# Moving a wait for gate rows and one load of turned rows at the start of the early units

## The chip, the cores and the metric

The kernel runs on one NeuronCore of one Trainium2 chip. A NeuronCore has five engines with instruction streams of their own: TensorE (PE; its weight loads are listed as PEld), VectorE (DVE), ScalarE (ACT), GpSimd (POOL) and SyncE (SP). They are ordered only by semaphores. Transfers are issued by SyncE, ScalarE (ACTq) and GpSimd (POOLq) and carried out by sixteen DMA engines. The metric is the device time of one execution in microseconds, smaller is better; the time of a kernel is the median of its runs.

## The reference

For x of shape (4, 1024, 512), 4096 tokens in all, a modulated layer: six rows per batch come from `silu(c) @ wmod`, two of them gates.

```python
h = _layernorm(x) * (1 + ca) + sa
x = x + ga * attn_ref(h, ...)      # shift-mix time part, then channel part
h = _layernorm(x) * (1 + cb) + sb
x = x + gb * ffn_ref(h, ...)       # gb: the gate rows of this case

# ffn_ref: D = 512, F = 352, E = 8 experts, K = 2, shared width 704 = 2 * F
shared = (silu(x @ Wsg.T) * (x @ Wsu.T)) @ Wsd.T
scores = softmax(x @ Wr.T);  top 2 of 8, weighted by their scores
out_e  = (silu(x @ Wg[e].T) * (x @ Wu[e].T)) @ Wd[e].T
return routed + shared
```

## The kernel before

The 4096 tokens are 32 tiles of 128 rows. Stage 1 (the time part) and stage 2 (the channel part, the second layer norm, router logits and routing) go tile by tile. The feed-forward part is cut into units. A unit is one half (352 columns) of the shared network for one tile, or one tile of 128 routed rows for one expert. In a unit TensorE does `up` (24 products of 128x352 in banks PS_G and PS_U), ScalarE the `silu`, VectorE `hid` (the product of both), TensorE turns `hid` (`rows_turned`, L2067), ScalarE and VectorE split it in a high and a low part (`hid_hi` L1225, `hid_lo` L1658), and TensorE does `down` (9 products, L2072 to L2074). Products are made of three matmuls each, from float32r high and low parts (L573 to L575), so every operand has a high and a low tile.

The units come in four parts. **Fused**: units 0 to 29, the shared network for tiles 0 to 14 (FU = 15), run inside the steps of stage 2, four steps behind (LAG). **Early**: tiles 15 to 18 (`EARLY`, up to SPLIT = 19), two units each, after stage 2 has ended. **Routed**: 39 double tiles of 256 rows, each with its expert's weights. **Late**: shared units of tiles 19 to 31. This case acts at the seam of fused and early.

A shared unit reads its rows in turned form from DRAM, where ScalarE stored them (`store_turned`, `h3T_out`), into one of two tiles `ex_x_hl`. Fused units use `ex_x_hl[1]` alone (`fused_turned`, semaphore `sf_in`, L1234). Early units alternate (`load_turned`, `sx_in`, L1239): tile 15 slot 0, tile 16 slot 1. Slot 0 lies on the bytes of `x2_t`, which stage 2 reads until `xhat_2` of tile 31 in step 29; unit n runs in step n + 4. ScalarE issues these loads in `silu_of`, after the activation of every second unit. TensorE waits for them in `up` (L2152).

The gate rows `mod3` are four rows of 512, one for each batch, spread over all partitions by four loads of SyncE (L871, semaphore `mod3_in`). VectorE first multiplies with them in `base_of` (L1828), for tile 15; tiles to 14 use another copy, `gb_t`, in `base_fused` (L1676, L1679).

What matters around this is the order of VectorE's queue in `early_step`, since an engine runs its queue strictly in order. In each half: `hid_lo` of the unit before; routing pieces of the last group of tiles (BEFORE_HID); `hid` of this unit; in the first half `base_fused` or `base_of` of the tile before; more pieces (AFTER_HID). The pieces end in `expert_tables`, `tile_tables` (L1789 to L1796, releases `route_done`) and `result_slots`.

SyncE's queue at the seam, in order: the last rows to be scattered (`load_scattered`, L844, which wait for earlier scatters `sc_out`, then L862), the gate rows L871, residual rows of tiles 15 and 16 (L877), the store of tile 14 (L894), residual rows of 17 and 18 (L877, each waits for the landing of the one two before it), two more row loads (L862), `route_done`, the first expert's weights (L626 to L629), eight stores of zero rows behind the experts' regions (`pad_rows`, L888, `pad_out`), then, after waits for all scatters and all zero rows, the first expert's rows (L911) and the second expert's weights. GpSimd issues the scatters (L1048, L1089). ScalarE's first routed step has `expert_hi` of the second expert (L1307) ahead of the second half of the rows (L1298) and of `hid_hi`.

Of the kernel before, what the change touches and what calls it, by code (L numbers as in the profile page):

```python
# [23 lines left out]
B, T = 4, 1024  # L24
N = B * T
NT = N // P
# [10 lines left out]
FU = 15  # L37
# [82 lines left out]
EARLY = Part(FU, SPLIT, 0, FUSED)  # L120
# [4 lines left out]
def slot_of(part, n):  # L125

    return (n - part.first) % 2
# [60 lines left out]
def in_fused(v):  # L188
    return v.real() and v.n < 2 * FU
# [35 lines left out]
def build(nc, io, out):  # L225
# [16 lines left out]
    with ctx:  # L242
        def sem(name):
            return ctx.enter_context(nc.semaphore(name))
# [4 lines left out]
        def steps(name, *names):  # L249
            return Steps(sem(name), *names)  # L250
# [215 lines left out]
        mod3_in = sem("mod3_in")  # L466
# [44 lines left out]
        xh2_vec = steps("xh2_vec", "xhat")  # L511
# [601 lines left out]
        def _(act):  # L1113
# [113 lines left out]
            def silu(u, bank, follows=True):  # L1227
                if follows:
                    act.wait_ge(*u_vec.done(u - 1, "hid"))
                act.wait_ge(*u_pe.done(u, "up"))  # L1230
                act.activation(sg_t[:], PS_G[bank][:, 0:F], ACT.Silu).then_inc(u_act.sem, 1)  # L1231

            def fused_turned(n):
                act.dma_start(ex_x_hl[1][:].rearrange("p m c t -> p (m c t)").bitcast(F32),  # L1234
                              h3T_d[n * P:(n + 1) * P, :]).then_inc(sf_in, 16)

            def load_turned(part, n):
                slot = slot_of(part, n)
                act.dma_start(ex_x_hl[slot][:].rearrange("p m c t -> p (m c t)").bitcast(F32),  # L1239
                              h3T_d[n * P:(n + 1) * P, :]).then_inc(sx_in[slot], 16)  # L1240
# [11 lines left out]
            def silu_of(v):  # L1252
                if not in_fused(v):
                    return
                silu(v.n, 0, v.back(1).real())
                if v.p == 0:
                    return
                if v.pair is None and v.n == 2 * FU - 1:
                    act.wait_ge(*xh2_vec.done(NT - 1, "xhat"))
                    load_turned(EARLY, FU)  # L1260
                    load_turned(EARLY, FU + 1)
                else:
                    fused_turned(v.half + 1)

            def route_ones_of(t):
                if t.n == 2:
                    act.wait_ge(route_const, 4)
                    act.activation(ones[:], ones_made[:], ACT.Copy).then_inc(route_ones, 1)
                    act.activation(earlier[:], earlier_made[:], ACT.Copy).then_inc(route_ones, 1)
# [119 lines left out]
        def _(dve):  # L1389
# [424 lines left out]
            def pieces(table, t, half):  # L1814
                for piece in table.get(2 * (t.n - FU) + half, ()):
                    piece(*([LAST] if piece in (softmax_and_first, second, row_slots) else []))

            def hid_of(part, t, half):
                dve.wait_ge(*u_pe.done(part.unit(t, half) - 2, "turned"))
                hid_rows(part.unit(t, half), half, bank_of(part, half))  # L1820

            def hidlo(part, t, half):
                hidlo_rows(part.unit(t, half))

            def base_of(part, n):
                dve.wait_ge(*u_pe.done(part.unit(part.tile(n), 1), "down"))
                dve.wait_ge(*base_vec.done(n - 1, "base"))
                dve.tensor_tensor(gated_t[:], PS_Y[:], mod3[:, n // TPB, :], ALU.mult).then_inc(base_vec.sem, 1)  # L1828
                order = n - FU
                dve.wait_ge(sr_in[order % 2], 16 * (order // 2) + 16)  # L1830
                if n >= 2 * COMBINED_FIRST:
                    dve.wait_ge(*cb_vec.done(n // 2, "out"))
                dve.wait_ge(*base_vec.done(n, "gated"))
                dve.tensor_tensor(base[:, n, :], base[:, n, :], gated_t[:], ALU.add).then_inc(base_vec.sem, 1)
# [19 lines left out]
            def early_step(t):  # L1854
                for half in range(2):
                    hidlo(*EARLY.before(t, half))
                    pieces(BEFORE_HID, t, half)
                    if t.only(SPLIT - 1) and half:
                        expert_lo(FIRST, 0)
                    hid_of(EARLY, t, half)  # L1860
                    if not half:
                        if t.only(FU):
                            base_fused(FU - 1, 2 * FU - 1, True)
                            dve.wait_ge(mod3_in, 16 * B)
                        else:
                            base_of(EARLY, t.n - 1)
                    pieces(AFTER_HID, t, half)
                if t.only(SPLIT - 1):
                    x_lo(0, 0)
# [81 lines left out]
        def _(pe):  # L1951
# [169 lines left out]
            def rank_in_step(t):  # L2121
                g = group_at(t.n, 2)
                if g is not None:
# [4 lines left out]
                    rank(g)  # L2128

            lead, _, before_rank = in_turn((r2, 0), (k2, 0), (fused_up, LAG), (tk, 0), (t3, 2), (fused_down, LAG), (cv, 0))  # L2130
            _, _, after_rank = in_turn((router, 2), (t2, -2))

# [147 lines left out]
```

## Time and profile before

| | us |
|---|---|
| median of 3 runs | 1848.51 (1846.16 to 1848.79) |
| the profiled execution | 1840.96 |
| its span | 1839.2 |
| TensorE busy in it | 1712.8 (93%), 9093 matmuls |
| VectorE busy | 1344.8 (73%) |
| ScalarE busy | 772.1 (42%) |
| GpSimd busy | 547.4 (30%) |
| DMA | 339.30 MB, mean 184 GB/s |
| mean granted TensorE clock | 0.971 of full speed |

The span runs from the first to the last instruction, the execution's time has 1.8 us more around it. Busy times overlap. A releaser in brackets is what ended an engine's idle time. The granted clock is either 1.00 (2.4 GHz) or 0.50 (1.2 GHz); a value between is a mean over a stretch. A DMA share is the busy share of the sixteen DMA engines, and can read a little over 1.

### The profile page before, as it was taken

What the parts mean: (1) busy time and instruction counts of PE and PEld (TensorE: products, weight loads), DVE (VectorE), ACT (ScalarE), POOL (GpSimd) and SP (SyncE); (2) the same over time, 40 slices, a digit from 0 to 9 for tenths busy, and PEclk for the clock granted to TensorE, in tenths of its full rate; (3) what the DMA queues carried; (4) which work ended last, traced back from release to release, by engine and by line L of the source; (5) the groups of instructions that cost most, each with busy time, mean ns of one, the idle gap of its engine ahead of it and who ended that gap; (6) DMA issues with size and microseconds to landing.
All of it is one profiled execution on the core that took longest, in us unless ns stands there. A gap on an engine that the chain in (4) does not pass through costs nothing.

```text
span 1839.2 us, 28387 instructions
## 1 busy us (share of the span) xinstructions
PE 1712.8 (93%) x9093; PEld 1485.2 (81%) x9093; DVE 1344.8 (73%) x2468; ACT 772.1 (42%) x1151; POOL 547.4 (30%) x631
## 2 busy tenths in 40 slices
PE   5499999999579999999999988999999999999998
PEld 0388888887468888888887878999999999998898
DVE  4899999995578778787877545666666767665872
ACT  2343333332245545454554313545455454542331
POOL 0244444442254433545554540000000000003740
PEclk9699999999889999999999979999999999999999
DMA  9432222221533443545454688677777777675861
GB/s 334 134 118 91 85 80 86 91 80 60 178 115 123 157 146 115 212 172 178 172 195 149 207 302 296 229 266 262 260 250 247 272 244 274 232 250 165 294 217 43
DMA packets 141638, 339.30 MB, mean 184 GB/s; under 512 B 20664, under 2 KB 20664, under 8 KB 136048
## 3 DMA queue, kind: packets, MB, share of 16 engines
q1 hardware_dynamic: 110864, 250.68, 39.8%
q10 hardware_dynamic: 20448, 54.01, 7.9%
q0 software_dynamic: 10240, 33.56, 5.3%
q8 instruction: 42, 0.69, 0.2%
q14 instruction: 44, 0.36, 0.1%
HBM read 230.40 MB, written 107.79 MB: 184 GB/s over the span
## 4 chain that ended last, share of the span: by engine, by line
PE 65%; DVE 19%; DMA 5%; issue 4%; POOL 3%; ACT 2%; SPq 1%; DVEq 0%; ACTq 0%; POOLq 0%
PE bank L573 16%; PE bank L575 16%; PE bank L574 16%; DVE mix L1570 5%; PE bank L584 4%; PE bank L2074 4%; PE bank L2072 4%; PE bank L2073 4%; PE bank L2067 2%; DVE xm_lo L1576 1%; ACT xm_hi L1173 1%; POOL diff L1017 1%; DMA stage<-in_w_k 1%; DVE hid L1654 1%; POOL raw L1107 1%
## 5 line engine op out<-in xcount | busy, mean ns | idle before, releaser
L573 PE MATMUL bank<-gu_hi,ex_x_hl 128*128 128x352 f32 x1136 | 380.7, 335 | 3.8 <-DMA ex_x_hl<-h_turned 2.0
L575 PE MATMUL bank<-gu_hi,ex_x_hl 128*128 128x352 f32 x1136 | 368.7, 325 | 0.0
L574 PE MATMUL bank<-gu_lo,ex_x_hl 128*128 128x352 f32 x1136 | 368.6, 324 | 0.0
L1107 POOL DMA_INDIRECT raw<-expert_out_rows,out_slots x64 | 73.9, 1154 | 596.6 <-DMA expert_out_rows<-y_rows 572.6
L1654 DVE TENSOR_TENSOR hid<-bank,sg_t 128x352 f32<-128x352 f32 x142 | 74.0, 521 | 200.4 <-ACT sg_t L1231 200.4
L573 PEld LDWEIGHTS bank<-gu_hi,ex_x_hl 128*128 128x128 f32 x1136 | 215.9, 190 | 4.4 <-DMA ex_x_hl<-h_turned 2.2
L574 PEld LDWEIGHTS bank<-gu_lo,ex_x_hl 128*128 128x128 f32 x1136 | 216.2, 190 | 0.0
L1570 DVE SCALAR_TENSOR_TENSOR mix<-diff,vecs,h2T 128x128 f32<-128x128 f32 x256 | 160.7, 695 | 75.6 <-POOL diff L1017 75.6
L575 PEld LDWEIGHTS bank<-gu_hi,ex_x_hl 128*128 128x128 f32 x1136 | 215.5, 190 | 0.0
L1231 ACT ACTIVATE sg_t<-bank 128x352 f32<-128x352 f32 x142 | 66.1, 466 | 273.5 <-PE bank L575 273.2
L2072 PE MATMUL bank<-dn_hi,hid_hi 128*128 128x512 f32 x426 | 170.3, 400 | 8.1 <-DVE hid_lo L1658 8.1
L2074 PE MATMUL bank<-dn_hi,hid_lo 128*128 128x512 f32 x426 | 168.7, 396 | 0.0
L2073 PE MATMUL bank<-dn_lo,hid_hi 128*128 128x512 f32 x426 | 167.4, 393 | 0.0
L1845 DVE TENSOR_TENSOR gu_lo<-raw,gu_hi 128x2816 fp32r<-128x2816 f32 x41 | 126.3, 3081 | 1.4 <-ACT gu_hi L1307 1.4
L1165 ACT ACTIVATE h2T<-bank,vecs 128x128 f32<-128x128 f32 x128 | 48.2, 457 | 177.6 <-PE bank L584 177.6
L573 PE MATMUL bank<-w_r_hi,xm_hi 128*128 128x512 f32 x256 | 108.1, 422 | 10.1 <-DVE h1T L1493 10.1
L1307 ACT ACTIVATE gu_hi<-raw 128x2816 fp32r<-128x2816 f32 x41 | 104.9, 2559 | 15.5 <-issue 10.2
L1225 ACT ACTIVATE hid_hi<-bank 128x384 fp32r<-128x384 f32 x142 | 68.7, 484 | 88.1 <-PE bank L2067 88.1
L574 PE MATMUL bank<-w_r_lo,xm_hi 128*128 128x512 f32 x256 | 104.4, 408 | 0.0
L575 PE MATMUL bank<-w_r_hi,xm_lo 128*128 128x512 f32 x256 | 104.2, 407 | 0.0
L573 PE MATMUL bank<-w_k_hi,xm_hi 128*128 128x512 f32 x256 | 103.9, 406 | 0.0
L1502 DVE SCALAR_TENSOR_TENSOR stage<-diff,vecs,h1T 128x128 f32<-128x128 f32 x384 | 102.9, 345 | 0.0
(231 smaller groups left out, 3941.0 us busy)
## 6 DMA issues: line engine op xcount, KB each, us to landing
raw<-in_ex_gu SPq DMA_DIRECT2D x39, 1408.0 KB, 6.8
raw<-in_ex_dn SPq DMA_DIRECT2D x39, 512.0 KB, 7.5
ex_x<-expert_in_rows SPq DMA_DIRECT2D x78, 256.0 KB, 2.8
expert_out_rows<-y_rows ACTq DMA_DIRECT2D x78, 256.0 KB, 4.2
h_rows<-h_t SPq DMA_DIRECT2D x64, 256.0 KB, 2.4
h_turned<-h_hl ACTq DMA_DIRECT2D x32, 512.0 KB
ex_x_hl<-h_turned ACTq DMA_DIRECT2D x32, 512.0 KB, 3.8
x_t<-in_x SPq DMA_DIRECT2D x32, 256.0 KB, 2.6
```

The lines of the kernel that those rows point to most:

```text
L573: pe.matmul(acc, act_hi[i], w_hi[i], start=(i == 0), stop=False)
L574: pe.matmul(acc, act_hi[i], w_lo[i], start=False, stop=False)
L575: last = pe.matmul(acc, act_lo[i], w_hi[i], start=False, stop=(i == chunks - 1))
L1107: pool.indirect_dma_start(rows[:, pair % 2, a, :], None, ys_d, bass.IndirectOffsetOnAxis(ap=out_slots[:, k, n:n + 1], axis=0)).then_inc(ar ...
L1307: act.activation(flat_of(gu_hi, t), raw[t.p][:, 0:C * GU], ACT.Copy).then_inc(rw_hi_act.sem, 1)
L1502: last = dve.scalar_tensor_tensor(mix1[:, m, c, :], diff1[:, c, :], vecs[:, mu, c:c + 1], h1T[:, t.p, c, 0:P], ALU.mult, ALU.add)
L1570: last = dve.scalar_tensor_tensor(mix2[:, m, c, :], diff2[:, c, :], vecs[:, mu, c:c + 1], h2T[:, t.p, c, 0:P], ALU.mult, ALU.add)
L1654: dve.tensor_tensor(hid[:, half, 0:F], PS_U[bank][:, 0:F], sg_t[:], ALU.mult).then_inc(u_vec.sem_of["hid"], 1)
L1845: dve.tensor_tensor(flat_of(w_lo, t), raw[t.p][:, cols], flat_of(w_hi, t).bitcast(F32), ALU.subtract).then_inc(rw_lo_vec.sem, 1)
L2072: pe.matmul(PS_Y[:], hid_hi[:, c, :], dn_hi[w][:, c, :], start=start and c == 0, stop=False)
L2073: pe.matmul(PS_Y[:], hid_hi[:, c, :], dn_lo[w][:, c, :], start=False, stop=False)
L2074: last = pe.matmul(PS_Y[:], hid_lo[:, c, :], dn_hi[w][:, c, :], start=False, stop=stop and c == FK - 1)
```

## The change

VectorE's wait for `mod3_in` leaves the first early step, where it stood behind `base_fused` of tile 14, and is put into `base_of` for tile 15 (n == FU), in front of the wait for that tile's `down`. In `silu_of` the load of tile 15's turned rows leaves unit 29 and goes to unit 27 (n == 2 * FU - 3), behind that unit's `fused_turned`, with its wait for `xhat` of tile 31. Unit 29 keeps only the load of tile 16's rows. The condition `v.pair is None` goes: these steps are all written out. No computing instruction and no transfer is added or taken away.

```diff
@@ -1255,12 +1255,13 @@
                 silu(v.n, 0, v.back(1).real())
                 if v.p == 0:
                     return
-                if v.pair is None and v.n == 2 * FU - 1:
-                    act.wait_ge(*xh2_vec.done(NT - 1, "xhat"))
-                    load_turned(EARLY, FU)
+                if v.n == 2 * FU - 1:
                     load_turned(EARLY, FU + 1)
                 else:
                     fused_turned(v.half + 1)
+                if v.n == 2 * FU - 3:
+                    act.wait_ge(*xh2_vec.done(NT - 1, "xhat"))
+                    load_turned(EARLY, FU)
@@ -1823,6 +1824,8 @@
             def base_of(part, n):
+                if n == FU:
+                    dve.wait_ge(mod3_in, 16 * B)
                 dve.wait_ge(*u_pe.done(part.unit(part.tile(n), 1), "down"))
                 dve.wait_ge(*base_vec.done(n - 1, "base"))
                 dve.tensor_tensor(gated_t[:], PS_Y[:], mod3[:, n // TPB, :], ALU.mult).then_inc(base_vec.sem, 1)
@@ -1861,7 +1864,6 @@
                         if t.only(FU):
                             base_fused(FU - 1, 2 * FU - 1, True)
-                            dve.wait_ge(mod3_in, 16 * B)
                         else:
                             base_of(EARLY, t.n - 1)
```

## Rows read from the trace of the kernel before

**Rows 1.** The chain of waits, 1040 to 1140 us: start, length, what.

```profile
1082.52 8.54 DMA mod<-mod_rows
...
1120.32 7.71 DMA expert_in_rows<-y_rows
...
1131.94 8.08 DMA raw<-in_ex_dn
```

**Rows 2.** Windows: stretch, length, busy PE, PEld, DVE, ACT, POOL, PEclk, DMA share, GB/s.

```profile
1068.00:1076.00 8.00, 5.99 (x28) 5.09 (x28) 5.55 (x21) 2.49 (x4) 4.34 (x6) 0.77 0.95 323
...
1084.00:1100.00 16.00, 11.68 (x60) 10.64 (x60) 4.82 (x23) 0.96 (x2) 8.49 (x9) 0.79 1.04 387
1100.00:1108.00 8.00, 7.08 (x41) 6.30 (x41) 5.99 (x17) 1.42 (x3) 4.39 (x4) 1.00 0.49 180
1108.00:1128.00 20.00, 18.91 (x110) 17.35 (x109) 6.59 (x13) 2.64 (x6) 0.00 (x0) 1.00 0.97 345
...
1150.00:1300.00 150.00, 150.00 (x899) 140.22 (x898) 102.16 (x113) 75.18 (x90) 0.00 (x0) 1.00 0.73 255
```

**Rows 3.** Timeline of TensorE: start, length, instruction, [idle before <-releaser].

```profile
1073.27 0.66 PE L573 MATMUL bank<-gu_hi,ex_x_hl 128*128 128x352 f32 x1 [1.99 <-DMA ex_x_hl<-h_turned]
...
1091.79 0.77 PE L2072 MATMUL bank<-dn_hi,hid_hi 128*128 128x512 f32 x1 [4.32 <-DVE hid_lo L1658]
...
1135.85 0.60 PE L584 MATMUL bank<-ident,ex_x 128*128 128x128 f32 x4
...
1144.39 0.50 PE L2072 MATMUL bank<-dn_hi,hid_hi 128*128 128x512 f32 x1 [1.65 <-DVE hid_lo L1658]
```

**Rows 4.** Timeline of VectorE, 1083 to 1107 us.

```profile
1091.09 0.56 DVE L1658 TENSOR_TENSOR hid_lo<-bank,hid_hi 128x384 fp32r<-128x384 f32 x1 [7.18 <-DMA mod<-mod_rows]
...
1102.40 0.69 DVE L1828 TENSOR_TENSOR gated_t<-bank,mod 128x512 f32<-128x512 f32 x1 [0.89 <-PE bank L2074]
1103.20 0.69 DVE L1834 TENSOR_TENSOR base<-base,gated_t 128x512 f32<-128x512 f32 x1
...
1106.66 0.18 DVE L1796 CAST row_of_tile<-row_f 128x39 int32<-128x39 f32 x1
```

**Rows 5.** Timeline of ScalarE and its DMA issues, 1042 to 1141 us.

```profile
1042.78 0.33 ACTq L1234 DMA_DIRECT2D ex_x_hl<-h_turned  x1
...
1067.43 0.81 ACTq L1239 DMA_DIRECT2D ex_x_hl<-h_turned  x2
...
1140.11 2.56 ACT L1307 ACTIVATE gu_hi<-raw 128x2816 fp32r<-128x2816 f32 x1 [1.59 <-DMA raw<-in_ex_dn]
```

**Rows 6.** Timeline of SyncE's DMA issues, 1075 to 1130 us (xN: N issues merged).

```profile
1075.89 2.69 SPq L844 DMA_DIRECT2D sc_rows<-h_rows  x2
...
1092.10 3.25 SPq L877 DMA_DIRECT2D base<-xres_rows  x2
1095.39 0.95 SPq L862 DMA_DIRECT2D sc_rows<-h_rows  x2
1107.97 0.35 SPq L626 DMA_DIRECT2D raw<-in_ex_gu  x1
...
1110.22 10.48 SPq L888 DMA_DIRECT2D expert_in_rows<-y_rows  x8
1128.81 0.94 SPq L911 DMA_DIRECT2D ex_x<-expert_in_rows  x2
```

**Rows 7.** Windows over three stretches at the lower clock, columns as in rows 2.

```profile
1058.30:1065.30 7.00, 6.98 (x29) 7.00 (x30) 4.87 (x15) 0.49 (x1) 3.14 (x3) 0.52 0.82 293
1073.20:1079.00 5.80, 5.73 (x19) 5.74 (x20) 3.04 (x16) 0.00 (x0) 0.00 (x0) 0.50 0.74 280
1091.70:1096.20 4.50, 4.41 (x12) 3.46 (x13) 1.73 (x9) 0.00 (x0) 1.93 (x2) 0.50 1.03 413
```

**Rows 8.** DMA, 1108 to 1128 us, in 40 slices of half a microsecond.

```profile
GB/s 270 360 446 318 270 406 383 406 428 338 311 107 156 188 283 250 315 389 385 406 414 410 401 414 406 406 410 406 406 410 406 406 418 406 401 410 385 315 156 8
```

## The prediction

> **What bounds the kernel now.** I read three views in this order. First the chain of waits between 1040 and 1140 us, the place where the change acts: it leaves TensorE and runs through transfers [rows 1]. It passes the gate rows' load (8.54 us), later the zero rows that SyncE writes behind every expert's region (7.71 us), and then the last piece of the second expert's weights (8.08 us). From 1150 us on, the windows show TensorE busy for all of 150 us [rows 2]: whatever is won before that point and still there at 1144 us is won at the end, since every later wait hangs on TensorE's own progress. So the question is what the change does to one instruction, TensorE's first L2072 behind 1142 us, which starts at 1144.39 [rows 3].
>
> Second, TensorE's timeline [rows 3]. At 1073.27 it has waited 1.99 us for the first early tile's turned rows. At 1091.79 it has waited 4.32 us for `hid_lo`. At 1144.39 it has waited 1.65 us for `hid_lo` again. VectorE's rows [rows 4] tell why at the second place: it stood 7.18 us for the gate rows before `hid_lo`. ScalarE's row tells why at the third: the conversion L1307, queued ahead of `hid_hi`, started at 1140.11 when the second expert's weights had landed [rows 5].
>
> Third, the transfers. SyncE issues the first expert's weights at 1107.97, right behind VectorE's table (L1796 at 1106.66, `route_done`), then eight zero-row stores from 1110.22 to 1120.70, and only at 1128.81, when these have landed, the first expert rows, with the second expert's weights behind them [rows 4, 6]. The sixteen DMA engines have a share of 0.97 in 1108 to 1128 and of 1.04 in 1084 to 1100, but of only 0.49 in between [rows 2]. So from 1108 on this chain is a matter of moving bytes, not of when SyncE starts alone.
>
> **Part 1, VectorE's wait for the gate rows moves to `base_of` of tile 15.** No instruction is added; the wait now stands in front of L1828 at 1102.40 instead of behind L1679. What was queued behind it was `hid_lo` of the first early unit, and behind that TensorE's L2072. The gate rows land at 1091.06 (1082.52 + 8.54) [rows 1], so VectorE and TensorE no longer stand there. TensorE wins its 4.32 us, and what the clock cost behind it: 4.5 us at a granted clock of 0.50, which is 1.2 GHz against 2.4, half of which is lost, 2.2 us [rows 3, 7]. Sum 6.5 us. At its new place the wait holds back the sum, the tables of `route_done` and the next `hid_lo`, in this order.
>
> **Part 2, tile 15's turned rows are loaded in unit 27.** The load leaves the pair of issues at 1067.43 and goes behind the one at 1042.78 [rows 5]. There ScalarE issues it beside an activation; its 512 KB have 28 us to land. The added wait on `xhat` is for something finished two steps earlier. I cost the move at nothing there; if the cover were gone, ScalarE's issue of 0.4 us (half of the 0.81 of the pair) would stand ahead of one activation. What it wins: TensorE's 1.99 us, and half of the 5.8 us at granted clock 0.50 behind it, 2.9 us [rows 3, 7]. Sum 4.9 us. Tile 16's rows, now alone, are wanted two units later and are not late.
>
> **Both together, up to the tables.** 6.5 + 4.9 = 11.4 us; the half-clock stretches also cover small gaps, so I use 11. L1828 would stand at 1102.4 - 11 = 1091.4, which is when the gate rows land (1091.06), and the sum L1834 at 1092.2, which is when tile 15's residual rows land: SyncE's L877 at 1092.10 was waiting for just that [rows 4, 6]. Both are met to within a few tenths. That is luck, and a wait of 0 to 2 us here is possible; it is covered, as follows. The tables would be ready at 1106.8 - 11 = 1095.8. SyncE itself is busy until 1096.34 with the rows L862 [rows 6], so the first weights go out at about 1097 instead of 1107.97.
>
> **What is late next.** The transfers. From 1097 the engines have work without a break. The work itself stays: in 1100 to 1108 it is 0.49 x 8 = 3.9 us of all sixteen engines, in 1108 to 1128 it is 0.97 x 20 = 19.4 us [rows 2]. Laid end to end from 1100 that is 23.3 us at full share, 1123.3, or 22.4 us at the share of 1.04 that the mixed stretch shows. Two bounds of one kind: the old end of 1128.0 moves by 4.7 to 5.6 us. If the mixture had gaps as in 1108 to 1128, it is 4.0. Part 2 adds something: 512 KB less between 1068 and 1076, at 323 GB/s 1.6 us of transfer, at a share of 0.95 [rows 2]. SyncE's row at 1075.89 waits for scatters of that stretch to land [rows 6], and what follows (rows, gate rows, residual rows) can go as much earlier, 0 to 1.6 us. In all 4.0 to 7.2 us; I take 5.7. Only the idle share between 1100 and 1108 can be used up, and it is used up as soon as the tables are done by about 1099: that is the cover of the 2 us above, and it means that most of the 11 us isn't needed.
>
> At one place a page bears on this. The Trainium skill, DMA: Bandwidth & Descriptors, section Issuing engines are not separate DMA queues, says that transfers from all engines run on the same sixteen DMA engines and interleave. It speaks against the change, since it leaves no second path for the weights and zero rows that start sooner; the shares of 0.97 and 1.04 agree [rows 2]. Its section Anatomy of one DMA gives bytes over 436 GB/s beside a fixed 2 us; by that rate the 9.5 MB of rival (b) would take an estimated 21.8 us, and the kernel would end near 1841.7; no stretch of [rows 2] reaches it.
>
> **From there to the end.** First expert rows would be asked for at 1128.81 - 5.7 = 1123.1, and be there some 3 us later. TensorE wants them at 1135.85 - 11 = 1124.9 [rows 3], so it waits a little over 1 us. The second expert's weights land at 1140.02 - 5.7, ScalarE's L1307 starts at 1134.4, and TensorE's L2072 at 1144.39 - 5.7 = 1138.7. TensorE's block before it ended at 1142.74 (1144.39 - 1.65). Moved by the 9.8 us that are left to it, it ends at about 1133, and TensorE idles 5 to 6 us there. That is a new and longer wait than any of the three now. Behind idle times of 1.99 and 4.32 us the granted clock stood at 0.50 for 5.8 and 4.5 us, and in 1058.30 to 1065.30 for 7 us [rows 7]. Half of such a stretch is lost: 2.2 to 3.5 us, and it isn't hidden, since TensorE is the bound from 1144 on. I take 2.4, near the row with the longest idle time before it; the ends are 0 (the clock stays) and 3.5.
>
> **The sum.** 5.7 - 2.4 = 3.3 us won; from 4.0 - 3.5 = 0.5 to 7.2 - 0. The profiled execution took 1840.96 us (span 1839.2 and 1.8 around it); its run was 7.5 us under the median of the three shown, 1848.51, and the gain is a difference in one stage, so I put it on the median: 1848.51 - 3.3 = 1845.2.
>
> **Rivals.** (a) The transfers are not what holds the zero rows back, and the whole 10.5 to 11 us reach the second expert's weights: 1838.0. For it speaks that everything in SyncE's queue is ordered from `route_done` on; against it the shares of 0.97 and 1.04, and that zero-row stores go out 1.3 us apart and the last still lands 7.71 us after its issue. (b) The mixture is moved at the best rate seen for long, about 410 GB/s [rows 8], not at the mean. Between 1097 and 1128 there are 3 us at 387 GB/s, 8 at 180 and 20 at 345 [rows 2], 9.5 MB together; they take 23.2 us from 1097, end 1120.2, 7.8 us sooner, less 2.4 for the clock, 5.4 won: 1843.1. For it: 387 GB/s in 1084 to 1100. Against: slices at 107 to 283 GB/s on the weights in the same row. (c) The other side: slower. The weights and zero rows now run beside the last scatters and the rows L862 that feed them. If small pieces of scattered rows and large ones together go at the rate of the poor slices [rows 8], some 250 GB/s, 9.5 MB take 38 us instead of 31 and the end comes 7 us later than 1128; less would do: below 307 GB/s (9.5 MB in 31 us) the end is later than now, and below about 294, 1.3 us later, the clock's 2.4 us make the kernel slower by 0.2%. At 280 GB/s, 34 us, it is 3 us late and the time 1848.5 + 3 + 2.4 = 1853.9. (d) The change doesn't do what it says, because the wait comes back at `base_of` or in the residual rows behind it and lasts over 3 us: then the tables come at 1099 or later, the gap in the transfers is only partly filled, and the gain of 1 us or two is eaten by the clock: 1848.5.
>
> **How the numbers follow.** What a measurement of this kernel can tell from no change is about 0.2%, 3.7 us. The forecast, with its bounds (1843.0 to 1848.0), has 0.70; (a) 0.12, (b) 0.10, (c) 0.04, (d) 0.04. Of the forecast's 0.70 some 0.24 lie over 3.7 us. Faster: 0.24 + 0.12 + 0.10 = 0.46. Slower: (c), and a rest for the bounds, 0.05. Within: 0.49. The range for 8 in 10 reaches down to (a), 1837.8, and up to 1848.5.
>
> **What would show it.** In the changed kernel: no idle time at the first L573 of the early units; `hid_lo` there released by ScalarE; VectorE at L1828 near 1091; SyncE's first weights near 1097; no gap in the DMA share between 1100 and 1108; the first expert rows issued near 1123; TensorE idle for 5 us or so before the L2072 near 1139, then a clock of 0.50 for some us. If the rows are issued near 1118, (a) is right. If TensorE's clock stays after its wait, the gain is 5 to 6 us. The prediction is wrong altogether if another wait than the second expert's weights ends last ahead of that L2072.

## The result: 12.5 us faster at first, 9.3 us over more runs

The changed kernel takes 1836.15 us (median of 4 runs, 1834.76 to 1836.90), the one before 1848.65 (4 runs, 1846.16 to 1850.95): ratio 0.9932, 95% interval 0.9915 to 0.9949. Run again beside 26 runs of the kernel before, it takes 1837.09 us (6 runs) against 1846.36: ratio 0.9949 (0.9932 to 0.9966). The medians differ by 12.5 us in the one comparison and by 9.3 in the other; 3.3 us were forecast, with 0.5 to 7.2 as its bounds. The two traced executions, 1840.96 and 1836.88, differ by 4.1 us only, and the rest of this document has to account for that too.

The traced execution took 1836.88 us, with a span of 1835.1. First the lines of the page (busy us of each engine, then the chain of waits by engine, for the whole kernel after the change).

```profile
span 1835.1 us, 28386 instructions
PE 1711.8 (93%) x9093; PEld 1484.5 (81%) x9093; DVE 1345.3 (73%) x2468; ACT 772.1 (42%) x1151; POOL 549.5 (30%) x631
PE 69%; DVE 17%; issue 4%; DMA 3%; POOL 3%; ACT 2%; SPq 1%; DVEq 0%; ACTq 0%; POOLq 0%
```

The windows of the changed kernel's seam, with the columns of [rows 2], whose stretches the first four repeat; the last is the 7 us behind TensorE's wait at the second expert.

```profile
1068.00:1076.00 8.00, 7.90 (x49) 7.30 (x49) 3.49 (x10) 2.96 (x5) 5.31 (x7) 0.99 0.83 303
1084.00:1100.00 16.00, 15.02 (x88) 13.72 (x87) 10.99 (x39) 2.38 (x5) 8.43 (x9) 1.00 1.04 404
1100.00:1108.00 8.00, 6.91 (x40) 6.14 (x39) 3.18 (x7) 0.96 (x2) 3.88 (x4) 1.00 1.00 363
1108.00:1128.00 20.00, 19.94 (x116) 18.22 (x114) 8.67 (x11) 5.32 (x7) 0.00 (x0) 1.00 0.83 312
...
1138.80:1145.80 7.00, 7.00 (x29) 6.02 (x30) 5.51 (x6) 2.35 (x3) 0.00 (x0) 0.68 0.44 126
```

The gap in the transfers, 0.49 in [rows 2], is gone (1.00). In 1068 to 1076 and in 1084 to 1100 TensorE is busy for 22.9 of 24 us, at a granted clock of 0.99 and 1.00. The timelines of TensorE, VectorE, ScalarE and SyncE of the changed kernel, beside [rows 3 to 6]:

```profile
1098.94 0.47 PE L2074 MATMUL bank<-dn_hi,hid_hi 128*128 128x512 f32 x1 [0.98 <-DVE hid_lo L1659]
1129.41 0.66 PE L584 MATMUL bank<-ident,ex_x 128*128 128x128 f32 x4 [1.47 <-DVE ex_x_hl L1841]
1138.74 0.79 PE L2074 MATMUL bank<-dn_hi,hid_hi 128*128 128x512 f32 x1 [4.51 <-DVE hid_lo L1659]
...
1093.88 0.69 DVE L1831 TENSOR_TENSOR gated_t<-bank,mod 128x512 f32<-128x512 f32 x1 [0.95 <-PE bank L2076]
...
1045.49 0.33 ACTq L1234 DMA_DIRECT2D ex_x_hl<-h_turned  x1
1045.85 0.44 ACTq L1239 DMA_DIRECT2D ex_x_hl<-h_turned  x1
1134.47 2.55 ACT L1308 ACTIVATE gu_hi<-raw 128x2816 fp32r<-128x2816 f32 x1 [4.46 <-DMA raw<-in_ex_dn]
...
1099.32 0.35 SPq L626 DMA_DIRECT2D raw<-in_ex_gu  x1
1101.71 12.62 SPq L888 DMA_DIRECT2D expert_in_rows<-y_rows  x8
1123.72 0.94 SPq L911 DMA_DIRECT2D ex_x<-expert_in_rows  x2
```

The wait of a little over 1 us that was forecast for the first expert rows did not come. TensorE turns them at 1127.34 without idle time. Its 1.47 us ahead of 1129.41 are for VectorE's split of the rows just turned, and the kernel before has the same wait:

```profile
1137.92 0.66 PE L584 MATMUL bank<-ident,ex_x 128*128 128x128 f32 x4 [1.47 <-DVE ex_x_hl L1838]
```

In absolute time nearly every other step stands where it was put: the first weights at 1099.3 (forecast 1097), the first expert rows at 1123.7 (1123.1), ScalarE's conversion at 1134.5 (1134.4), TensorE's matmul at 1138.74 (1138.7), behind a wait of 4.5 us (5 to 6), and the clock falls behind it (0.68 in the window above). And yet the medians say 9 us or more, not 3.3. The two traces do not enter the seam at the same time.

### The profile page after: what moved, and what is told of

It is laid out like the page before. It is cut to its first block, busy times and chain, and to the rows that moved or that the text cites. A ratio compares the mean times of both kernels' runs of the same rounds, so it can differ in the third digit from the quotient of the medians.

```text
span 1835.1 us, 28386 instructions
## 1 busy us (share of the span) xinstructions
PE 1711.8 (93%) x9093; PEld 1484.5 (81%) x9093; DVE 1345.3 (73%) x2468; ACT 772.1 (42%) x1151; POOL 549.5 (30%) x631
## 4 chain that ended last, share of the span: by engine, by line
PE 69%; DVE 17%; issue 4%; DMA 3%; POOL 3%; ACT 2%; SPq 1%; DVEq 0%; ACTq 0%; POOLq 0%
PE bank L573 17%; PE bank L574 17%; PE bank L575 17%; DVE mix L1571 5%; PE bank L584 4%; PE bank L2076 4%; PE bank L2074 4%; PE bank L2075 4%; PE bank L2069 2%; DVE xm_lo L1577 1%; ACT xm_hi L1173 1%; POOL diff L1017 1%; DMA stage<-in_w_k 1%; DVE k_lo L1584 1%; DVE hid L1655 1%
```

## Counting from one common instruction

The first matmul of the last routing group (`bank<-route_hot,earlier`) is the same in every version. The wait that the change moves lies behind it. The moved load is issued 15.2 us ahead of it (1045.85), but does not shift it: ScalarE's issue just before that load, L1234, stands 15.54 us ahead of the point in the kernel before (1042.78) and 15.55 in the changed one (1045.49). TensorE's timeline, the kernel before, then the changed one:

```profile
1058.32 0.26 PE L2114 MATMUL bank<-route_hot,earlier 128*128 128x40 f32 x1 [1.88 <-DVE route_hot L1725]
```

```profile
1061.04 0.26 PE L2116 MATMUL bank<-route_hot,earlier 128*128 128x40 f32 x1 [1.90 <-DVE route_hot L1726]
```

The changed kernel's execution came 2.7 us later to this point, and it was 2.7 us later at L1234 already. Over all the traces below the point lies at 1057.6 to 1061.5 us, in kernels with the moved load (1058.1 to 1061.5) and without it (1057.6 to 1061.4) alike. So I count from it. The far end is VectorE's 41st `hid<-bank,sg_t`, from which on everything goes by TensorE; the kernel before, then the changed one:

```profile
1158.68 0.53 DVE L1654 TENSOR_TENSOR hid<-bank,sg_t 128x352 f32<-128x352 f32 x1 [2.66 <-ACT sg_t L1231]
```

```profile
1155.08 0.52 DVE L1655 TENSOR_TENSOR hid<-bank,sg_t 128x352 f32<-128x352 f32 x1 [2.66 <-ACT sg_t L1231]
```

From there to the end of the span are 1839.2 - 1158.7 = 680.5 us in the one and 1835.1 - 1155.1 = 680.0 in the other: nothing is given back later. So the 4.1 us between the two executions are 6.3 us won between the two points, 2.7 lost ahead of them and 0.5 won behind. The agreement in absolute time above is luck by these 2.7 us: counted from the point the forecast put the first weights at 38.7, the expert rows at 64.8 and TensorE's down at 80.4, and they stand at 38.3, 62.7 and 77.7. All positions below are starts, in us from the common instruction; "down" is TensorE's first matmul with `hid_hi` for the second expert, in brackets its wait.

| kernel | gate rows issued | first weights | expert rows | down | 41st hid |
|---|---|---|---|---|---|
| before | 22.20 | 49.65 | 70.49 | 86.07 (1.65) | 100.36 |
| before, again | 21.99 | 50.40 | 72.90 | 88.08 (2.77) | 103.97 |
| before + copy | 22.24 | 50.05 | 71.75 | 86.92 (2.00) | 101.22 |
| load alone | 19.97 | 48.69 | 70.76 | 86.96 (3.34) | 103.81 |
| wait alone | 21.88 | 40.98 | 64.90 | 80.62 (4.73) | 97.27 |
| after | 19.68 | 38.28 | 62.68 | 77.70 (4.51) | 94.04 |
| after, again | 19.71 | 38.13 | 61.72 | 77.01 (3.97) | 93.79 |
| after + copy | 19.76 | 38.30 | 65.08 | 80.53 (5.75) | 97.22 |
| after, tables late | 18.46 | 41.47 | 64.64 | 79.94 (3.26) | 96.89 |
| after, clock kept | 19.92 | 38.24 | 62.03 | 77.74 (0.76) | 92.02 |
| before, order changed | 22.02 | 51.98 | 73.80 | 86.73 (0) | 104.79 |
| after, order changed | 20.05 | 38.71 | 62.15 | 73.33 (0) | 91.35 |
| after, order on both | 20.03 | 38.77 | 63.01 | 73.03 (0) | 88.09 |

## Experiments

The theories at the outset: does the excess come from how executions of one kernel differ, outside the stretch that the change acts on, or from that stretch itself (the seam, 1058 to 1150 us); and within the seam, is it the bytes or the order of the issues that sets the expert rows.

### Both kernels once more, unchanged

> The kernel before, unchanged, run under a name of its own. Its profiled execution took 1840.96 us, its timed runs 1846 to 1851, and the changed kernel 1834.8 to 1836.9 with a profiled execution of 1836.88. Theory S (the seam gains 4 us and the executions of before differ among themselves): a new profile of the same kernel differs from the old one by up to 10 us in span, in stalls that lie outside the seam at 1060 to 1150 us, and the ratio to the kernel before is 1.000 within 0.002. Theory M (the gate rows usually land later than in the one trace read): the new profile shows VectorE standing 10 us or more before the hid_lo of the first early unit, where it was 7.18 us, and everything ahead of 1060 us is the same.

> The changed kernel, unchanged. Theory S: its new profile can differ from the old one by as much as the two of before differ; seam as in the first trace (TensorE's first down behind the last early unit at 103 to 105 us behind the last fused unit's turn). Theory M: the profile stays within 2 us of the first, since no wait for the gate rows is left; ratio 0.993, in 1834 to 1838 us where before takes 1846 to 1851.

Measured: before again 1.0001 (0.9989 to 1.0013), after again 0.9949 (0.9932 to 0.9966). The 26 runs of the kernel before lie between 1840.39 and 1852.96 us, and one of them is below the traced 1840.96 on which the forecast rests, so that was an unusually quick execution. The new trace of the kernel before took 1845.56. TensorE, VectorE and a window (columns as in [rows 2]) of it:

```profile
1093.48 0.76 PE L2072 MATMUL bank<-dn_hi,hid_hi 128*128 128x512 f32 x1 [8.12 <-DVE hid_lo L1658]
1146.55 0.50 PE L2072 MATMUL bank<-dn_hi,hid_hi 128*128 128x512 f32 x1 [2.77 <-DVE hid_lo L1658]
...
1092.78 0.56 DVE L1658 TENSOR_TENSOR hid_lo<-bank,hid_hi 128x384 fp32r<-128x384 f32 x1 [10.97 <-DMA mod<-mod_rows]
...
1148.00:1152.00 4.00, 4.00 (x18) 3.52 (x17) 3.38 (x4) 2.10 (x3) 0.00 (x0) 0.62 0.40 110
```

VectorE stood 10.97 us for the gate rows, not 7.18, since it came to them earlier: TensorE had waited only 0.78 us for the first early tile's turned rows here, not 1.99, and kept more of its clock behind (0.78 in 1073.4 to 1079.2, not 0.50 as in [rows 7]). The gate rows themselves landed 1.5 us later, counted from the common instruction (1092.78 - 1058.47 against 1091.09 - 1058.32). Behind the second wait (2.77, not 1.65) TensorE's clock fell, which it had not done in the first trace. From the common point to the 41st `hid` this execution took 103.97 us, 3.6 more than the first: 2.0 at the down, 1.6 behind it with the fallen clock. The theory that put the excess outside the seam falls for the larger part: of the 4.6 us between these two executions 3.6 arise inside it. That does not hold of every pair of traces: over all thirteen, the common point lies within 3.9 us and the stretch behind the 41st `hid` takes 678.3 to 682.4 us. The other theory, that the gate rows usually land later, is right in its sign (1.5 us), but the first weights went out only 0.75 us later.

Two later runs bear it out, since what they change acts only behind the gate rows. VectorE in the kernel before with the copy and in the one with the order changed:

```profile
1092.10 0.56 DVE L1662 TENSOR_TENSOR hid_lo<-bank,hid_hi 128x384 fp32r<-128x384 f32 x1 [10.13 <-DMA mod<-mod_rows]
```

```profile
1095.97 0.56 DVE L1662 TENSOR_TENSOR hid_lo<-bank,hid_hi 128x384 fp32r<-128x384 f32 x1 [10.94 <-DMA mod<-mod_rows]
```

From the common point that is 33.8 and 34.5 us, where the first trace has 32.8. TensorE's waits at the two early places were 1.99 and 4.32 us in the first trace, 0.78 and 8.12 in the second, 1.20 and 7.27 with the copy, 1.07 and 8.09 with the order changed. The first trace, from which the change was priced, is the odd one.

### Each half alone

The wait alone, against the kernel before:

```diff
+                if n == FU:
+                    dve.wait_ge(mod3_in, 16 * B)
...
-                            dve.wait_ge(mod3_in, 16 * B)
```

The load alone:

```diff
-                if v.pair is None and v.n == 2 * FU - 1:
-                    act.wait_ge(*xh2_vec.done(NT - 1, "xhat"))
-                    load_turned(EARLY, FU)
+                if v.n == 2 * FU - 1:
...
+                if v.n == 2 * FU - 3:
+                    act.wait_ge(*xh2_vec.done(NT - 1, "xhat"))
+                    load_turned(EARLY, FU)
```

> Only VectorE's wait for the gate rows is moved; the turned rows of tile 15 stay in unit 29. By the chain of transfers (the step of the prediction): the tables come 6.5 us sooner, that is enough to fill most of the gap in the transfers between 1100 and 1108, so the expert rows are issued 3 to 4 us sooner and 1 to 2 us are left after the clock. By theory S the timed ratio is that plus nothing: 0.998 to 1.000. By theory M nearly the whole measured gain is here: ratio 0.993 to 0.995.

> Only the load of tile 15's turned rows is moved to unit 27; VectorE's wait for the gate rows stays. TensorE's wait of 1.99 us at the first early up is gone and its clock may stay up, but VectorE then stands 4 to 5 us longer for the gate rows, which come when they come: by the chain of transfers at most 0 to 1.6 us are won (SyncE's chain starts sooner by the transfer that left 1068 to 1076): ratio 0.999 to 1.000. By theory M the same. A ratio under 0.997 would say that the gain comes from this part and the reason of both theories is wrong.

Measured: the wait alone 0.9971 (0.9956 to 0.9985), 5.9 us between the medians. That lies between what the two theories gave (0.998 to 1.000 and 0.993 to 0.995), and its expert rows go out 5.6 us sooner than in the first trace of the kernel before and 8.0 sooner than in the second, where 3 to 4 were expected. The load alone 0.9996 (0.9983 to 1.0009), 1.8 us between the medians and not to be told from nothing. Together they give 9.3. TensorE's timeline with the load alone, at the place of [rows 3]:

```profile
1092.81 0.76 PE L2073 MATMUL bank<-dn_hi,hid_hi 128*128 128x512 f32 x1 [7.86 <-DVE hid_lo L1659]
```

The load brings TensorE and VectorE to the gate rows sooner, and there they stand longer (7.86 us, not 4.32): what it wins is lost at the next wait. In the second trace of the kernel before TensorE stands there just as long (8.12), since the turned rows were nearly in time. The load also starts SyncE's chain of rows sooner: gate rows are issued at 18.5 to 20.1 in the eight traces with the moved load, and at 21.9 to 22.2 in the five without. Little of that is left while VectorE stands at its old place (first weights at 48.69, not 49.65 and 50.40; rows at 70.76, not 70.49 and 72.90), and more without that wait: between wait alone and after, the first weights go out 2.7 us sooner.

### A copy of 1408 KB in SyncE's queue, in either kernel

One more transfer, of the size of a weight piece, which nothing reads, is issued shortly before `route_done`; SyncE needs 0.65 us for it. All else is computed as before.

```diff
+            sp.dma_start(extra_d[:], io["ex_gu"][0]).then_inc(extra_out, 16)
             sp.wait_ge(route_done, 1)
...
+            sp.wait_ge(extra_out, 16)
```

> The kernel before with one more transfer, 1408 KB from DRAM to DRAM by one issue of SyncE, put just ahead of its wait for route_done, so where the DMA share was 0.49. Nothing reads it. Theory T (the moved bytes set when the zero rows have landed, and the gap between 1100 and 1108 is spare): the transfer of some 3.5 us of all sixteen engines goes into the gap; the share there rises to 0.9 or more, the first expert rows are issued within 1 us of where they were, counted from the last fused unit, and the time is that of the kernel before within 0.1%. Theory O (the order of SyncE's issues from route_done on sets it, the bytes do not): the same here, 0 us.

> The changed kernel with the same transfer at the same place in SyncE's queue. Here the engines have a share of 1.0 from there on. Theory T: the first expert rows are issued 3 to 4 us later than in the changed kernel, and the whole kernel is 3 to 4 us slower than the changed one (ratio to before 0.996 to 0.998 where that has 0.995). Theory O: 0.4 us for one issue, ratio unchanged at 0.995.

Measured: in the kernel before, 1.0006 (0.9991 to 1.0021); in the changed kernel, 0.9969 (0.9956 to 0.9981), 2.9 us above the changed kernel's 1837.09. The intervals of 0.9969 and of 0.9949 overlap, so that the traces have to decide. Windows behind the copy, the kernel before with it, then the changed one with it (columns as in [rows 2]):

```profile
1100.35:1108.65 8.30, 7.48 (x43) 6.69 (x42) 6.34 (x18) 1.42 (x3) 4.07 (x4) 1.00 0.88 324
```

```profile
1100.62:1108.92 8.30, 8.30 (x51) 7.88 (x50) 2.93 (x5) 1.32 (x3) 3.73 (x4) 1.00 0.92 363
```

In the kernel before, the copy goes into the gap (share 0.88 where it was 0.49) and costs nothing; its expert rows go out at 71.75, between the two traces without it (70.49 and 72.90). In the changed kernel the gap is used up and the same copy puts the rows off by 2.4 and 3.4 us against the two traces of it, more than SyncE's 0.65 us. So the expert rows wait for bytes, and rival (a), by which the transfers hold nothing back, is refuted, although its time (1838.0) was the nearest of all. The Trainium skill, DMA: Bandwidth & Descriptors, section Issuing engines are not separate DMA queues, says that transfers share the sixteen DMA engines whoever issues them. By that rule a copy costs nothing where the engines are idle and time where they are busy, and both runs agree. They don't test its "whoever": the copy stands in SyncE's own queue, and no run here adds a transfer of another engine at this place.

### The tables 3 us later

```diff
+                for _ in range(5):
+                    link(dve.memset(y_rows[:, 1, :], 0.0))
```

> The changed kernel with five memsets of 128x512 one behind the other on VectorE, ahead of the tables that release route_done (about 3 us). Theory T: the engines still have 3 to 4 us of older work when the first weights would be issued, so the first expert rows come at most 1 us later and the time is within 0.1% of the changed kernel. Theory O: rows, second weights and end are 3 us later, ratio to before 0.9965 instead of 0.995.

Measured: 0.9965 (0.9952 to 0.9978), 2.6 us above the changed kernel, with an interval that overlaps that of 0.9949. It is the number of the theory by which order alone decides, which the copy refutes. The windows of 4.7 us ahead of the first weights, the changed kernel, then this one:

```profile
1094.62:1099.32 4.70, 3.72 (x23) 3.41 (x23) 4.33 (x13) 0.55 (x2) 1.70 (x2) 1.00 1.02 399
```

```profile
1095.19:1099.89 4.70, 0.54 (x3) 0.33 (x2) 4.18 (x14) 0.46 (x1) 0.84 (x1) 0.98 0.74 292
```

First weights 3.2 us later (41.47 against 38.28), rows 2.0 and 2.9 us later, 41st `hid` 2.9 and 3.1. So the start counts beside the bytes: a later start leaves a new gap in the transfers (0.74). The run is not a clean one for TensorE: the five fills also stand ahead of the next `hid_lo`, TensorE waits 4.17 us for it at 1099.52 (0.98 in the changed kernel), and its wait for the second expert is shorter for that (3.26). The expert rows do not pass TensorE, and they tell. The forecast's cover, by which tables until 1099 cost nothing, is wrong.

### The clock kept up

While TensorE waits for the second expert it computes 24 further matmuls that nobody reads.

```diff
+                    if t.only(0) and not half:
+                        for _ in range(2):
+                            product(pe, PS_RT[:, 0:F], chunks_of(ex_x_hi[0]), ...)
```

> The changed kernel with 24 products of 128x352 whose result nobody reads, into a bank that is unused there, ahead of the last early down in TensorE's queue: 3.8 us of work in a wait of 4.0 to 4.5 us. If the clock falls because of this wait and costs 2 us behind it (the step of the prediction): the down starts when it did, the granted clock stays 1.00, and the next hid comes 2 us sooner; ratio to before 0.994 where the changed kernel has 0.995. If the products push the down back (the wait is shorter than they are) the two cancel. If the clock falls nevertheless, the wait isn't the cause: nothing changes.

Measured: 0.9942 (0.9925 to 0.9959), 3.0 us under the changed kernel's 1837.09; the two ratios' intervals overlap. The trace is clearer. TensorE, and the window behind its wait:

```profile
1138.66 0.50 PE L2074 MATMUL bank<-dn_hi,hid_hi 128*128 128x512 f32 x1 [0.76 <-DVE hid_lo L1659]
...
1139.00:1146.00 7.00, 7.00 (x43) 6.53 (x42) 5.39 (x6) 2.65 (x4) 0.00 (x0) 1.00 0.33 94
```

The down stands at 77.74 as in the changed kernel (77.70), the granted clock stays at 1.00, and the 41st `hid` comes at 92.02, 1.8 to 2.0 us sooner. That is the price of the fallen clock; 2.4 was taken. What this execution won beyond that came behind the 41st `hid` (678.3 us to the end, not 680.0), where nothing was changed.

### The order in ScalarE's queue

`hid_hi` of the first expert's last tile is issued ahead of the second expert's conversion (L1307), so that it no longer stands behind the weights.

```diff
-                    expert_hi(t.back(-1), half)
+                    behind = t.only(0) and not half
+                    if not behind:
+                        expert_hi(t.back(-1), half)
...
+                    if behind:
+                        expert_hi(t.back(-1), half)
```

> The changed kernel, with ScalarE's conversion of the second expert's gate and up weights (L1308) put behind the second half of the rows, hid_hi and the silu of the first routed unit, in that one step; it waits for the weights there alone. Both theories on the transfers say the same of the rows. If TensorE's wait of 4.0 to 4.5 us ahead of the last early down is due to this order in ScalarE's queue, it goes; TensorE then runs one unit further before it needs the second expert's weights, waits 0 to 3 us there, and the clock stays at its upper level or falls for less: 3 to 7 us faster than the changed kernel, ratio to before 0.991 to 0.993. If something else holds hid_lo back: no change, 0.995.

> The kernel before with ScalarE's reordering of e8 and nothing else. Three traces of kernels with the wait for the gate rows in its old place had TensorE waiting 1.65 to 3.34 us ahead of the last early down, and in two of them the clock fell behind it. Theory W (that wait, and the clock behind it where it falls, is all that the order costs in the kernel before): 1.6 to 3.3 us of wait and up to 3.5 us of clock go, ratio 0.997 to 0.999. Theory V (the reordering wins what it won on the changed kernel, 4 us): ratio 0.998 too, but then TensorE has no wait at all up to the second expert's first unit and the seam ends 4 us sooner than in each of the traces of before. If the change and the reordering simply add up, this ratio times 0.995 is that of e8, 0.993.

Measured: in the changed kernel 0.9931 (0.9907 to 0.9956), 1832.93 us, 4.2 under the changed kernel alone, with intervals that overlap, and 2.4 to 2.7 us sooner at the 41st `hid`; in the kernel before 0.9997 (0.9984 to 1.0009), nothing, where 0.997 to 0.999 was expected. In the first, the down needs no wait at all (at 73.33) and a wait of 2.09 us is left for the next one. In the second, ScalarE's conversion started at 87.35, later than in any other trace. TensorE's timeline there, then ScalarE's, and ScalarE's in the changed kernel with the order changed:

```profile
1096.68 0.76 PE L2076 MATMUL bank<-dn_hi,hid_hi 128*128 128x512 f32 x1 [8.09 <-DVE hid_lo L1662]
1157.07 0.47 PE L2076 MATMUL bank<-dn_hi,hid_hi 128*128 128x512 f32 x1 [2.09 <-DVE hid_lo L1662]
```

```profile
1148.42 0.47 ACT L1231 ACTIVATE sg_t<-bank 128x352 f32<-128x352 f32 x1 [3.19 <-PE bank L575]
1148.78 2.56 ACT L1307 ACTIVATE gu_hi<-raw 128x2816 fp32r<-128x2816 f32 x1
```

```profile
1133.29 0.47 ACT L1231 ACTIVATE sg_t<-bank 128x352 f32<-128x352 f32 x1 [3.18 <-PE bank L575]
1133.65 2.56 ACT L1308 ACTIVATE gu_hi<-raw 128x2816 fp32r<-128x2816 f32 x1
```

The wait only moves one step on, to 95.6, and the clock falls behind it. The conversion did not wait for weights there: it follows the `silu` that now stands ahead of it, and that `silu` waits for TensorE. In its old place the conversion starts 10.7 to 11.9 us behind the issue of the expert rows, in the kernels before and after alike. Here it starts 13.6 us behind it, since TensorE comes later to the products that the `silu` waits for (3.19 us); in the changed kernel it starts 11.8 us behind it (73.95), as late as in its old place. So the new order puts the conversion off in the kernel before, and hardly in the changed one. Besides, this execution was late before the order could act (first weights at 51.98). How the lost and won time divides between the two, one trace doesn't tell.

### The order on both engines

As the one before, in the changed kernel, and `hid_lo` of that tile ahead of VectorE's part of the conversion too.

```diff
+                    if t.only(0) and half:
+                        expert_lo(t.back(-1), 0)
...
-                    expert_lo(t.back(-1), half)
+                    if half or not t.only(0):
+                        expert_lo(t.back(-1), half)
```

> The kernel of e8, and on VectorE the low part of the second expert's gate and up weights behind the hid_lo of the first routed unit instead of ahead of it. In e8 TensorE waited 2.09 us for that hid_lo and the clock fell for 3.4 us. Expected: this wait goes, one of about 1.2 us takes its place at the turn of the unit behind it (its hid is now behind the 3.08 us of the weights), the clock stays: 1 to 2.5 us faster than e8, ratio to before 0.992. If the weights' low part is now late for the second expert's first unit, 0 to 1 us slower than e8.

Measured: 0.9924 (0.9907 to 0.9940), 1830.74 us (1829.10 to 1832.19) against 1845.55. TensorE and VectorE at the second expert:

```profile
1141.14 0.52 PE L2076 MATMUL bank<-ident,hid 128*128 128x128 f32 x3 [0.67 <-DVE hid L1659]
...
1146.16 0.53 DVE L1659 TENSOR_TENSOR hid<-bank,sg_t 128x352 f32<-128x352 f32 x1 [1.84 <-ACT sg_t L1231]
```

The wait is down to 0.67 us and the 41st `hid` stands at 1146.16 - 1058.07 = 88.1, 5.7 and 5.9 us ahead of the two traces of the changed kernel. Of all the versions run it has the lowest time.

## Why the prediction was wrong

**What held.** The start: the first weights go out 11.4 us sooner, counted from the common point, and 11 were forecast. The chain: transfers, expert rows, the second expert's weights, ScalarE's conversion, `hid_lo`, TensorE. The moved load costs nothing in its new place (an issue of 0.44 us at 1045.85, and nothing up to the common point, as shown above). The waits of 1.99 and 4.32 us are gone with their slow stretches. VectorE found the gate rows there: its 0.95 us ahead of L1831 is for TensorE. The gap in the transfers closed, and a new wait of 4.0 to 4.5 us came up, with a fall of the clock behind it. TensorE's work ahead of that wait ended 11.2 us sooner, not 9.8, since it did not wait for the first expert rows.

**Step 1, "What is late next", was mis-sized.** It put the expert rows 5.7 us sooner (4.0 to 7.2). Counted from the common point they go out 7.8 and 8.8 us sooner than in the trace it was made from, and 10.2 and 11.2 sooner than in the second trace of the kernel before. The runs with the order changed, on one engine or both, and the one with the clock kept up act only behind this place and can be counted in: then the rows go out at 70.5, 72.9 and 73.8 in three executions without the change and at 61.7 to 63.0 in five with it, 10 us sooner in the mean. Windows from the common point to the first weights and from there to the expert rows (columns as in [rows 2]), the kernel before, its second trace, the wait alone, and the changed kernel:

```profile
1058.32:1107.97 49.65, 41.82 (x203) 38.38 (x204) 23.64 (x81) 8.06 (x14) 24.74 (x26) 0.79 0.82 290
1107.97:1128.81 20.84, 19.75 (x113) 18.03 (x112) 7.09 (x14) 2.87 (x6) 0.00 (x0) 1.00 0.93 332
```

```profile
1058.47:1108.87 50.40, 40.00 (x203) 36.80 (x204) 23.47 (x81) 8.06 (x14) 24.02 (x26) 0.83 0.81 287
1108.87:1131.37 22.50, 21.41 (x123) 19.48 (x122) 7.82 (x15) 3.02 (x7) 0.00 (x0) 1.00 0.86 306
```

```profile
1057.61:1098.59 40.98, 38.43 (x203) 35.60 (x204) 23.76 (x81) 8.07 (x14) 20.43 (x22) 0.88 0.88 312
1098.59:1122.51 23.92, 22.83 (x132) 20.90 (x131) 9.13 (x17) 4.45 (x8) 3.88 (x4) 1.00 0.93 357
```

```profile
1061.04:1099.32 38.28, 36.62 (x203) 34.17 (x204) 23.70 (x81) 8.07 (x14) 20.12 (x22) 0.91 0.89 322
1099.32:1123.72 24.40, 23.31 (x135) 21.37 (x134) 9.14 (x17) 4.92 (x8) 3.88 (x4) 1.00 0.92 347
```

Share times length is the transfers' own work, the rest is idle share. Before: 0.82 x 49.65 + 0.93 x 20.84 = 60.1 us of work in 70.5, 10.4 idle. Its second trace: the same work, 60.2, in 72.9, 12.7 idle. After: 0.89 x 38.28 + 0.92 x 24.40 = 56.5 us of work in 62.7, 6.2 idle. Of the 7.8 us from the first to the last, 4.2 are idle share and 3.6 are work. Against the second trace it is 6.5 us of idle share and 3.7 of work. The shares are given to 0.01, so each sum of work is known within 0.35 us. The forecast said that "Only the idle share between 1100 and 1108 can be used up" (4.1 us). Against the trace it was made from that much did go; against the second more went, and the whole stretch had 10 to 13 us of it to give. What the forecast had too small against its own trace is the work. The moved load takes 0.5 MB out of the stretch (21.3 MB before, 20.8 after, from the GB/s of the windows); 0 to 1.6 us were allowed for it. The remaining 2 us are the same bytes in less time: the wait alone moves 21.3 MB as before, but in 0.88 x 40.98 + 0.93 x 23.92 = 58.3 us of work. So full share was worth 21.3 / 60.1 = 355 GB/s before and 366 with the wait moved. Why the mixture is moved faster once it runs together, no run tells.

**Step 2, the clock term, was right in size, and in part no new cost.** From the down to the `hid` before the 41st are 1152.00 - 1144.39 = 7.6 us before and 1148.41 - 1138.74 = 9.7 after: 2.1 us, and 1.8 to 2.0 by the run that keeps the clock up. But three of the five traces of kernels in which VectorE's wait stood at its old place lose clock there as well: in the second trace of the kernel before behind 2.77 us of waiting (0.62 in 1148 to 1152), with the load alone behind 3.34 (0.61 in 1147.7 to 1154.7), with the order changed behind 2.09 (0.75 in 1157.1 to 1164). The first trace (1.65) and the one with the copy (2.00) are the two that do not. Two of the three that lose it carry a change of their own; of the three executions that had neither the load nor the order changed, one lost it. So part of the term is no new cost and should not have been taken off the median; how large a part, three traces don't tell.

**Step 3, "so I put it on the median", was the error that joined them.** It set a difference of two single executions against a median. Trace against trace, the seam won 100.36 - 94.04 = 6.3 us (8.4 to the down, less 2.1 for the clock). Against the second trace of the kernel before it won 9.9 to 10.2, and between the medians it is 9.3. The first trace came from one of the kernel's quickest executions, and its seam was 3.6 us shorter than that of the second. A difference worked out from it falls short of the difference of the medians by about 3 us (9.3 - 6.3), as far as the interval of 0.9949 (6 to 13 us) lets one say. That "the gain is a difference in one stage" did not protect from that, since most of the spread between those two traces is in that very stage.

**The cover was wrong too:** that "most of the 11 us isn't needed", and that it is enough for the tables to be done by about 1099, fell with the tables run late. Of the 11.4 us by which the first weights start sooner, the last 3.2 alone bring the rows 2.0 to 2.9 us forward. 7.8 us reach the expert rows, and the stage between first weights and rows gets longer by 3.6, since 3 us more of transfers' work now lie in it (22.4 us, not 19.4), the last scatters among them (GpSimd is busy for 3.88 us in it, not 0).

**The rivals.** (a) gave the nearest time by a mechanism that the copy refutes. (b) put the end of the transfers 7.8 us sooner, which is what the rows measured against the first trace, and was right that the rate rises; but 410 GB/s was not reached (347 from the first weights to the rows, 368 at full share), and half of the 7.8 is idle share. (c) did not come up: no slowdown by the mixture. (d) neither: the wait did not come back at `base_of`.

**Open.** The traces and 26 runs bound how the kernel before spreads, not why its gate rows land 1.0 to 1.8 us later in the other executions than in the first. The 12.5 us of the first comparison against the 9.3 of the second lie within their intervals.

## What to carry to other kernels

A seam in which several engines meet over shared transfers is to be read from more than one execution: compare the traced time with the runs around it first, and where it is lower than nearly all of them, expect its waits to be untypical (here one was longer and two were shorter than in the next trace). Do not charge a change with a cost before it is seen that the kernel before does not pay it in its other executions. And for the transfers, sum share times length from a common point ahead of the change to the instruction that waits for them, since idle share lies all along that stretch and not in the visible gap alone.

## What the runs showed of the chip

The length of one wait does not tell whether TensorE's clock falls behind it. It fell behind 1.99 us [rows 3, 7] (0.50) and behind 2.09 in the kernel before with the order changed (0.75 in 1157.1 to 1164), and stayed behind 2.00 us, in the kernel before with the copy. TensorE and the window behind, of that kernel:

```profile
1145.24 0.50 PE L2076 MATMUL bank<-dn_hi,hid_hi 128*128 128x512 f32 x1 [2.00 <-DVE hid_lo L1662]
...
1145.30:1150.00 4.70, 4.70 (x28) 4.27 (x29) 4.60 (x5) 2.35 (x3) 0.00 (x0) 1.00 0.93 316
```

And 26 executions of one kernel differ by up to 12.6 us (1840.39 to 1852.96), more than the 9.3 us that the change is worth beside them.
